# Causal maxima of the self-attention: the mask moves from a TensorE product to a VectorE add-and-maximum

## The reference, cut to what matters

```python
q, k, v = (qkv[0], qkv[1], qkv[2])
scores = jnp.einsum('bhqd,bhkd->bhqk', q, k) / np.sqrt(HD).astype(np.float32)
causal = jnp.triu(jnp.ones((s, s), dtype=bool), 1)
scores = jnp.where(causal[None, None], -jnp.inf, scores)
attn_w = jax.nn.softmax(scores, axis=-1)
attn = jnp.einsum('bhqk,bhkd->bhqd', attn_w, v)
```

## Time and profile before

| | us |
|---|---|
| median of 3 runs | 955.22 |
| the three runs | 949.08, 955.22, 955.23 |
| the profiled execution | 942.79 |
| its span, first to last instruction | 941.1 |
| mean granted TensorE clock in it | 0.973 of full speed |

### The profile page before, as it was taken

One profiled execution on the slowest core, in us unless ns is written; L12 is line 12 of the kernel. 1 busy time (PEld: TensorE's weight loads), 2 busy tenths in 40 slices (PEclk: granted clock), 3 DMA queues, 4 the chain that ended last, 5 costly groups with the idle time before them and its releaser, 6 DMA issues. The chain is left out here.

```text
span 941.1 us, 11162 instructions
## 1 busy us (share of the span) xinstructions
PE 881.2 (94%) x3920; PEld 536.5 (57%) x3920; DVE 580.7 (62%) x872; ACT 485.4 (52%) x705; POOL 176.2 (19%) x206
## 2 busy tenths in 40 slices
PE   4889999999999987999999999998888899999998
PEld 3556555555555434444445878774335667777775
DVE  3578756756877317277778874464554656556554
ACT  2523666565566653566664765436544424454332
POOL 9411233233122311000002350000015600000000
PEclk9989999999999997999999999997997999999999
DMA  4042243343354116000000000113646100000000
GB/s 138 15 76 48 45 81 56 74 77 65 70 107 80 37 36 242 0 0 1 0 1 2 20 0 1 34 35 82 128 94 177 49 1 24 1 1 23 0 23 23
DMA packets 21879, 46.28 MB, mean 49 GB/s; under 512 B 7896, under 2 KB 10840, under 8 KB 21440
## 3 DMA queue, kind: packets, MB, share of 16 engines
q1 hardware_dynamic: 19136, 43.17, 20.4%
q10 hardware_dynamic: 2080, 1.27, 0.6%
q0 software_dynamic: 608, 1.12, 0.5%
HBM read 17.03 MB, written 2.29 MB: 21 GB/s over the span
## 5 line engine op out<-in xcount | busy, mean ns | idle before, releaser
L1143 DVE TENSOR_REDUCE part_max<-psum 128x4 f32<-128x512 f32 x288 | 185.5, 686 | 76.3 <-PE psum L1643 57.2
L852 ACT ACTIVATE prob<-psum 128x1024 f32<-128x1024 f32 (+1 forms) x192 | 145.5, 809 | 85.5 <-PE psum L1665 85.0
L1643 PE MATMUL psum<-k,nat_hi 128*128 128x512 f32 x288 | 118.5, 452 | 6.5 <-DVE part_max L1143 5.0
L1665 PE MATMUL psum<-q,k 128*128 128x512 f32 (+3 forms) x384 | 96.8, 354 | 1.4 <-ACT prob L852 1.4
L1032 ACT ACTIVATE silu<-psum,wt_bias 128x512 f32<-128x512 f32 x64 | 40.5, 684 | 108.2 <-PE psum L358 94.3
L1643 PEld LDWEIGHTS psum<-k,nat_hi 128*128 128x128 f32 x288 | 51.6, 190 | 66.3 <-issue 52.9
L1682 PE MATMUL psum<-prob,vq 128*32 128x512 f32 (+3 forms) x768 | 81.8, 498 | 1.3 <-POOL prob L690 1.2
L690 POOL TENSOR_SCALAR_AFFINE_SELECT prob<-prob 128x256 f32<-128x256 f32 x128 | 52.3, 416 | 155.9 <-ACT prob L852 154.6
L1665 PEld LDWEIGHTS psum<-q,k 128*128 128x128 f32 x384 | 65.0, 189 | 22.3 <-ACT prob L852 11.6
L1514 DVE TENSOR_TENSOR masked_lo<-masked,masked_hi 128x1024 fp32r<-128x1024 f32 x32 | 41.9, 1311 | 40.8 <-ACT masked_hi L1039 40.8
L356 PE MATMUL psum<-tree_hi,wt_hi 128*128 128x512 f32 x128 | 53.9, 421 | 5.1 <-issue 3.5
(11 more groups left out here) (167 smaller groups left out, 1616.4 us busy)
## 6 DMA issues: line engine op xcount, KB each, us to landing
k<-nat_hi SPq DMA_DIRECT2D x92, 64.0 KB, 2.3
xq<-xq_b SPq DMA_DIRECT2D x36, 128.0 KB
q<-nat_hi SPq DMA_DIRECT2D x32, 128.0 KB, 2.3
wt<-in_wt SPq DMA_DIRECT2D x8, 512.0 KB, 4.2
nrm<-in_xT SPq DMA_DIRECT2D x4, 512.0 KB, 5.4
k<-nat_lo SPq DMA_DIRECT2D x32, 64.0 KB, 2.3
q<-nat_lo SPq DMA_DIRECT2D x16, 128.0 KB, 2.3
nrm<-stage SPq DMA_DIRECT2D x32, 64.0 KB, 2.3
```

The costliest lines, as they stand in the source:

```text
L852: act.activation(prob[:, s % 2, p, :, q0:CH], psum[:, 2 * p:2 * p + 2, q0:CH], ACT.Exp, scale=SCALE)\
L1143: dve.tensor_reduce(part_max[:].rearrange("q (j p i) k -> q p j i k", j=2, p=2)[:, :, :, i, kt], bank(5 + unit_slot[n, u] % 3).rearrange(" ...
L1643: mm = pe.matmul(heads, rounded(nat_hi[:, m, i * P:(i + 1) * P]), k1[:, qd, :, kt * P:(kt + 1) * P], start=True, stop=i != kt)
L1665: mm = pe.matmul(bank(2 * p + j)[:, q0:CH], k2[:, qd, p, j, kt * P:(kt + 1) * P], q2[:, qd, p, c * CH + q0:(c + 1) * CH], start=True, stop ...
```

## The change

The mask product of the diagonal units goes, and with it the two bf16 tiles and the two copies that filled them. For a diagonal unit VectorE now runs one `tensor_tensor_reduce` for each of the four heads. It reads the head's 128 x 128 scores in PSUM and `caus_f` in SBUF, adds them, writes the sum back over the scores in PSUM, and gives their maximum, started from -3e38, to one column of `part_max`. The other 28 units of a quad keep their single reduction.

```diff
+                if i == kt:
+                    for p in range(2):
+                        for j in range(2):
+                            at = (2 * p + j) * P
+                            ins = dve.tensor_tensor_reduce(
+                                psum[:, 5 + unit_slot[n, u] % 3, at:at + P],
+                                psum[:, 5 + unit_slot[n, u] % 3, at:at + P], caus_f[:], 1.0, -3e38,
+                                ALU.add, ALU.max, accum_out=part_max[:, 16 * j + 8 * p + i, kt:kt + 1])
+                    ins.then_inc(mx_free, 1)
+                    return
...
-                mm = pe.matmul(heads, rounded(nat_hi[:, m, i * P:(i + 1) * P]), k1[:, qd, :, kt * P:(kt + 1) * P],
-                               start=True, stop=i != kt)
-                if i == kt:
-                    mm = pe.matmul(heads, ident_b[:],
-                                   causal_b[:].rearrange("q (h k) -> q h k", h=1).to_broadcast([P, 4, P]),
-                                   start=False, stop=True)
-                mm.then_inc(mx_ps, 1)
+                pe.matmul(heads, rounded(nat_hi[:, m, i * P:(i + 1) * P]), k1[:, qd, :, kt * P:(kt + 1) * P],
+                          start=True, stop=True).then_inc(mx_ps, 1)
...
-            pool.tensor_copy(ident_b[:], ident[:])
-            pool.tensor_copy(causal_b[:], caus_f[:])
```

More of the change, by code:

```diff
@@ L92, in layer @@
         ident = sb("ident", [P, P])
-        ident_b = sb("ident_b", [P, P], BF16)
         caus_f = sb("caus_f", [P, P])
-        causal_b = sb("causal_b", [P, P], BF16)
         vbias = sb("vbias", [P, D])
```

## The result

The changed kernel's median is 943.92 us over 20 runs (939.17 to 952.85), against 950.36 us for the kernel before over its own 20 (939.98 to 955.23). The ratio is 0.9952, with a 95% interval of 0.9931 to 0.9972: a small gain, 4.6 us by the ratio, where I had forecast a loss of 2.4. An unaltered copy, run later beside the experiments, gave 935.63 us against 945.37 and a ratio of 0.9903 (0.9872 to 0.9934).

The account below looks back on a forecast made before the run. TensorE was taken to bound a quad, with small VectorE slack. Quads gain 2.2 us and the part where VectorE leads loses 4.6, so +2.4 us on the median 955.22 gives 957.6 us, range 947 to 976.

Parts of the forecast that it names:

- X: Joint pitch of a diagonal unit's four VectorE instructions; 0.61 us before, taken as 1.35, bounded by 0.84 and 2.0.
- What is added: Step pricing VectorE's new diagonal instructions: 0.265 us main plus 0.08 for the maximum, 0.345 a head.
- The table: Whole-kernel effect at other X: 1.0 gives -6 us, 1.65 gives +10, 2.0 gives +27.
- the second rival: On VectorE's diagonals: instruction cheap, X 0.84 to 1.1, TensorE stays the bound; 4 to 10 us faster; chance 0.15.
- Its sign: Mark of the cheap instruction in the new profile: quads last under 29.8 us.
- The sum: Step adding -2.2 us in quads and +4.6 where VectorE leads: +2.4, put on the median 955.22.
- The third rival: On TensorE, the mask product lay in a gap weight loads leave anyway; +11 us, 966 us; chance 0.05.
- The three places of the stalls: TensorE waits in a quad: 0.7 us at the turn, 0.6 at unit (n + 2, 2), about 0.3 at unit 23.
- the turn: Point at the end of step 8 where TensorE waits for VectorE's gather; forecast stall 0.7 us.
- the part where VectorE leads: Seven early diagonals, in n = 0, before the first gather and in n = 1, cost 0.74 us each: +4.6 net.
- VectorE's sum: VectorE's work in a quad, 18.3 + 8X us; fills the old 30.9 at X = 1.57, where VectorE becomes the bound.

Follow-up runs that it names:

- e1: Changed kernel with VectorE's four instructions taken out: diagonal units have no mask in the maxima and use the old single reduction; 930.88 us, ratio 0.9861.
- e4: Changed kernel with two of the four heads' instructions of each diagonal issued twice, six in all; 955.44 us, ratio 1.0118.
- the mixture: Changed kernel, but units 35 and 0 of each quad keep the mask product on TensorE and the single reduction; 935.21 us, ratio 0.9891.
- e5: Changed kernel with the turn and VectorE's negate one unit later, behind unit (n + 2, 2); 938.18 us, ratio 0.9919.
- e6: Changed kernel with VectorE's scaling of two constant columns moved from the start to just before the first maximum; ratio 0.9901.

## Why the prediction was wrong, step by step

The failed step is the choice of X in "What is added". I took 1.35 us; it is 0.96. The instruction is the three-input form that I priced at 0.265 us pipelined, and it takes 0.25. I added 0.08 us a head for putting out the maximum "pipelined". That step exists, with a row of 140 ns, but it starts together with the next head's instruction, and the pitch of 0.25 us, which holds whatever it costs, is already below the 0.265 of the main instruction alone. 4 x 0.08 is most of the 0.39 between 1.35 and 0.96; pipelining a little tighter than row less 0.075 is the rest. The rule of the Trainium skill, "VectorE: DVE Perf Modes", section "Two Vector instructions with no wait between them", that an accumulator output is a second instruction was right, and my turning it into a price was not. The estimate from the figures of the same page's section "The TRN2 errata", 1.03 us and about 5 us of gain, came closest.

The table had a line for this: X = 1.0 gives -6 us. Measured at equal clock and start, -3.6 in the traces and some -4 in the spans. So the second rival, the cheap instruction, is what happened, to which I gave 0.15. Its sign, quads under 29.8 us, did not come: they last 30.0, between its mark and the forecast's 30.5 to 31, because the stalls cost more than the table had for this X.

The absolute figure failed at a second step, in "The sum": I added the change to 955.22 us, the median of only three runs. Twenty runs of the same kernel give 950.36. So of the 13.7 us between the forecast 957.6 and the measured 943.92, 4.9 are the kernel before, and 8.8 the effect: +2.4 forecast, -6.4 by the two medians (-4.6 by the ratio), with the long start in every run of the changed kernel. Even the table's -6 would have read 949 us.

What was right. TensorE is the bound of a quad, and a mask product costs it 0.23 us (0.236 in e1, not 394 ns). The third rival falls. The three places of the stalls are where they were said to be, and e1 beside the changed kernel shows them to be nearly the whole cost of a steady quad. TensorE's waits for VectorE grew from 5.0 us to 4.7 + 3.7 for maxima and 2.3 at the turn, 10.7 together, at the lower end of the 10 to 20 forecast. The two copies on GpSimd cost nothing: the first unit came at the same distance from the first product (39.14 - 8.18 = 30.96 before, 45.99 - 15.05 = 30.94 after).

What was mis-sized in the table. At X near 1.0 I had -1.2 us a quad; it is -0.87, since TensorE's lost time at the three places is about 1 us where I had 0.65. For the part where VectorE leads I had +2.1 us; in the copy, unit 13 of n = 1, behind the diagonals that I counted there, starts on TensorE 1.0 us later than before (93.01 against 91.98). From there to the output projection the change gains 4.6 us where the table has 8.3. The two errors have opposite signs but don't cancel: -6 us in the table, -3.6 in the traces. At larger X the table is too mild: 5 to 7 us against 11 at 1.46, 27 against 42 at 1.96, or some 36 without what goes with the lower clock there. I had let VectorE's sum decide "from X = 1.57"; e4, at 1.46, already takes 32.3 us a quad with a sum of 30.0. Dense diagonals on a ring of three banks stall both engines in turn long before the sums are level (no run has another number of banks, so the ring's share in this is argued, not shown). A straight line between the measured points at 0.96 (-4 us) and 1.46 (+11 us) gives some 8 us at X = 1.35 where I had 2.4. It is an upper estimate, since the cost grows faster at larger X; no run stands at 1.35.

Unforeseen altogether was the start. It is no part of the change, but it moved the profiled execution by more than the change did.

## What to carry to other kernels

Before pricing an instruction by adding its rows, ask where the next one starts: rows of one engine overlap, and a small follow-up row may be nearly free. Where two engines hand over through a short ring, don't compare their sums over a period; walk the densest place, and treat it separately, as the mixture does. When a change of half a per cent is measured, first set spans against granted clock, run by run: groups of runs at one clock betray an effect that is not the change's.

## What the runs showed of the hardware

- `tensor_tensor_reduce` on 128 x 128 from PSUM, written back to PSUM, starts every 0.25 us (row 320 ns). Its accumulator read has a row of 140 ns and starts with the next instruction; behind a read the pitch is 0.25 us, without one 0.21, so it may cost 0.04 us.
- A scaling of 128 x 2 from SBUF to SBUF on VectorE was held by GpSimd's memsets of 6.9 us until the end of the first (rows of 1.55 to 1.75 us) or of the second (8.43 and 8.48 us), depending on whether it got in between the two; a reduction and a two-input add of SBUF data ran beside the same memset in 0.37 and 0.68 us. What decides whether it gets in stays open: it arrived at 6.24, 6.28, 6.31, 6.38, 6.41, 6.43 and 6.44 us in the traces where it did, at 6.37 and 6.42 where it didn't.
- Why the copy of the changed kernel was granted a higher clock than before in those runs (0.978 against 0.971) stays open; in e5 and e6, with the same work on TensorE, the medians were 0.971 and 0.974.
